# Three element-wise operations of a state-space layer with a quantized MLP, moved from GpSimd to VectorE

## What is computed

```python
xn = layernorm(x)                                    # x: 4 x 2048 x 2048, f32
s  = ((scan(xn) + xn * Dp) * sigmoid(xn @ Wg + bg)) @ Wo
def bit_linear(x, w, b, dim_in):
    x_norm = simple_rms_norm(x, dim_in)              # row / rms(row) / sqrt(dim_in)
    x_q = activation_quant(x_norm)                   # round(x * 127 / max|row|), back to scale
    w_q = sign(w) * mean(abs(w))
    return x_q @ w_q.T + b
h  = gelu(bit_linear(xn, w1, b1, 2048))              # 2048 -> 8192
g  = silu(bit_linear(h,  w2, b2, 8192))              # 8192 -> 2048
out = x + s * g
```

## Time and profile before

| quantity | value |
| --- | --- |
| runs of the kernel before | 3167.06 and 3173.94 us, median 3170.5 us |
| the profiled execution's own time | 3172.91 us |
| span of its slowest core, core 3 | 3171.3 us |
| spans of all cores | 3150.4 to 3171.3 us |
| busy in that span | PE 1671.7, DVE 1452.8, ACT 936.9, POOL 593.2 us |

### The profile page before, as it was taken

How to read it: one execution, slowest core, us unless ns; L and a number is a source line. 1 busy time by engine, 2 the same in 40 slices (tenths; PEclk the granted TensorE clock), 3 DMA queues, 4 the chain that set the end, 5 groups by cost and what they waited for, 6 DMA issues and landing times.

```text
span 3171.3 us, 23059 instructions; the slowest of 8 cores (3150.4 to 3171.3 us)
## 1 busy us (share of the span) xinstructions
PE 1671.7 (53%) x6432; PEld 649.0 (20%) x6432; DVE 1452.8 (46%) x1416; ACT 936.9 (30%) x1045; POOL 593.2 (19%) x264
## 2 busy tenths in 40 slices
PE   2222264555418747777777777600000079999933
PEld 1100021111103313323333222200000024444411
DVE  3655526777713312222222222279999623333354
ACT  2211008777701100012222222211111264645122
POOL 0000004555510000013333333333333100000000
PEclk9999995565559968878888888855555589999955
DMA  4100027777760151122222222133333355555155
GB/s 121 54 27 27 0 31 164 159 173 168 166 111 3 24 96 40 40 94 104 92 90 106 100 106 100 73 113 113 119 113 116 142 186 199 191 174 193 41 159 173
DMA packets 129723, 340.84 MB, mean 107 GB/s; under 512 B 17664, under 2 KB 68992, under 8 KB 114080
## 3 DMA queue, kind: packets, MB, share of 16 engines
q1 hardware_dynamic: 114144, 287.78, 26.5%
q0 software_dynamic: 15456, 51.58, 10.0%
HBM read 290.10 MB, written 100.66 MB: 123 GB/s over the span
## 4 chain that ended last, share of the span: by engine, by line
PE 44%; DVE 18%; DMA 14%; issue 12%; ACT 5%; another core or an unknown queue 3%; SPq 1%; DVEq 1%; POOL 0%; ACTq 0%; POOLq 0%
PE pmA L821 15%; PE pmA L1017 14%; PE pmA L736 4%; DMA p_s<-s1Tsc 4%; PE pmA L700 4%; DMA p_w<-w1T 3%; DMA s1Tsc<-p_w 3%; DVE p_t L950 3%; DVE p_t L957 2%; PE pmC L401 2%; ACT p_w L614 1%; DVE p_v L954 1%; DMA out<-p_og 1%; ACT p_dmp L605 1%
## 5 line engine op out<-in xcount | busy, mean ns | idle before, releaser
L1017 PE MATMUL pmA<-p_k2g,p_s 128*128 128x512 bf16 x2048 | 460.3, 381 | 489.1 <-ACT p_s L1006 489.1
L821 PE MATMUL pmA<-k1T,p_s 128*128 128x512 bf16 x2048 | 483.8, 395 | 169.4 <-DMA p_s<-s1Tsc 169.4
L1017 PEld LDWEIGHTS pmA<-p_k2g,p_s 128*128 128x128 bf16 x2048 | 191.6, 98 | 758.9 <-issue 550.0
L846 POOL TENSOR_TENSOR p_acs<-p_acs,p_h 128x1024 f32<-128x1024 f32 x63 | 213.2, 3384 | 432.3 <-ACT p_h L836 432.3
L821 PEld LDWEIGHTS pmA<-k1T,p_s 128*128 128x128 bf16 x2048 | 199.1, 101 | 455.1 <-issue 259.1
L829 DVE TENSOR_TENSOR p_h<-pmA,p_a1b 128x512 f32<-128x512 f32 x128 | 88.5, 692 | 381.4 <-PE pmA L821 381.4
L1031 DVE TENSOR_TENSOR p_S<-p_S,pmA 128x1024 f32<-128x1024 f32 x112 | 136.8, 1222 | 260.5 <-PE pmA L1017 260.5
L832 ACT ACTIVATE p_hg<-p_h,p_b1c 128x512 f32<-128x512 f32 x128 | 92.4, 722 | 458.6 <-DVE p_h L829 458.5
L961 DVE SCALAR_TENSOR_TENSOR p_k<-p_t,p_int 128x1024 bf16<-128x1024 f32 x64 | 210.2, 3285 | 11.3 <-DVE p_t L957 11.2
L944 POOL TENSOR_TENSOR p_v<-p_hg,p_c2b 128x1024 f32<-128x1024 f32 x64 | 150.6, 2354 | 305.7 <-DVE p_t L957 276.5
L582 PE MATMUL pmA<-ehl,bsel_t 32*128 32x512 bf16 x256 | 110.8, 572 | 175.9 <-DVE p_d L589 165.3
(11 more groups left out here) (161 smaller groups left out, 1818.7 us busy)
## 6 DMA issues: line engine op xcount, KB each, us to landing
p_w<-w2T SPq DMA_DIRECT2D x64, 1024.0 KB, 5.5
p_w<-w1T POOLq DMA_DIRECT2D x64, 512.0 KB, 8.6
s1Tsc<-p_w SPq DMA_DIRECT2D x256, 128.0 KB, 6.5
p_s<-s1Tsc SPq DMA_DIRECT2D x16, 2048.0 KB, 8.8
hgsc<-p_hg SPq DMA_DIRECT2D x64, 512.0 KB, 2.7
p_hg<-hgsc SPq DMA_DIRECT2D x64, 512.0 KB, 3.6
p_xb<-x_sh SPq DMA_DIRECT2D x16, 1024.0 KB, 7.3
k2Tsc<-p_k SPq DMA_DIRECT2D x64, 256.0 KB, 2.1
```

The source lines that it names most:

```text
L821: bld.op(TE, lambda e, k=k, icl=icl, tc=tc, pb=pb, sb_=sb_: e.matmul(pb[:, 0:512], sb_[:, k * 512 + icl * 128:k * 512 + (icl + 1) * 128], ...
L846: bld.op(GP, lambda e, h2b=h2b: e.tensor_add(acs[:], acs[:], h2b[:]), reads=[(h2b, 0), (h2b, 1), (acs, 0)], writes=[(acs, 0)])
L1017: bld.op(TE, lambda e, ic=ic, ds=ds, tc=tc, pb=pb, kg=kg, s2b=s2b: e.matmul(pb[:, tc * 512:(tc + 1) * 512], s2b[:, ic * 2048 + ds * 128:ic ...
```

## The change

The sum over squares (L841 and L846) and the multiplication by `c2b` (L944) go from GpSimd (`GP`) to VectorE (`VE`). Operands, types, shapes and the place of each call in the code stay as they were, and with them the line numbers.

```diff
                     if ic == 0:
-                        bld.op(GP, lambda e, h2b=h2b: e.tensor_copy(acs[:], h2b[:]),
+                        bld.op(VE, lambda e, h2b=h2b: e.tensor_copy(acs[:], h2b[:]),
...
                     else:
-                        bld.op(GP, lambda e, h2b=h2b: e.tensor_add(acs[:], acs[:], h2b[:]),
+                        bld.op(VE, lambda e, h2b=h2b: e.tensor_add(acs[:], acs[:], h2b[:]),
...
-                bld.op(GP, lambda e, hgb=hgb, vb=vb: e.tensor_mul(
+                bld.op(VE, lambda e, hgb=hgb, vb=vb: e.tensor_mul(
                     vb[:], hgb[:], c2b[:]),
```

## The result

| | before | changed |
| --- | --- | --- |
| median | 3169.7 us (19 runs) | 3194.1 us (20 runs) |
| ratio, 95% interval | | 1.0069 (1.0053 to 1.0085) |
| spans of all cores in the profiled execution | 3150.4 to 3171.3 us | 3169.9 to 3187.4 us |
| busy, slowest core: DVE, POOL | 1452.8, 593.2 us | 1467.5, 228.0 us |

The changed kernel is 0.7% slower: the ratio stands for 22 us (17 to 27), the medians lie 24.3 us apart; the forecast was +25.1 us and 3196 us. In five executions of the changed kernel, and in some of other kernels, cores of one die ran at a lower granted clock and took some 1 to 2% longer; the medians in the table hold them, while the ratio and every median from here on leave them out (the changed kernel's is then 3192.8 us).

What follows compares the result with a forecast made beforehand. VectorE's chain was taken to bound the rounding stage, TensorE's work and weight waits the Gelu stage. Rounding stage +27.5, head −1.1 and tail −1.3 gave +25.1 us, forecast 3196 us, range 3180 to 3216.

Steps and rivals of the forecast that it cites:

- VectorE no longer held by GpSimd: Rounding stage: with L944 off GpSimd, L961 stops waiting and the period falls from 6.82 to 4.67 us, 2.15 per chunk.
- What is added: Rounding stage: L944, two hand-overs and ScalarE's L947 join VectorE's chain, 2.56 us per chunk, making the period 7.23 us.
- Head and tail: Shorter first L944 at the rounding stage's head, −1.1 us; earlier release of `acs` at the Gelu stage's end, −1.3 us.
- Rival A: Rounding stage: round trip to ScalarE stays hidden, 5.82 us per chunk, −64 us, 3107 us; chance 0.04.
- Rival B: Rounding stage: L961's 3.39 us is its own cost, period 9.39 us, +164 us, 3335 us; chance 0.03.
- Gelu stage: First-half L829 comes 1.2 us late against 7.1 us of room, second half has 0.8 us to spare: cost nothing.
- Rival C: Gelu stage: the accumulations hold L829 until TensorE lacks a bank, 1.15 us per chunk, +74 us, 3270 us; chance 0.05.

Runs made afterwards that it cites:

- the three doses: Kernel before, GpSimd's c2b multiplication left out (but for two chunks), replaced by a copy, or kept: periods 4.68, 5.50 and 6.79 us; the first two took 3034.0 and 3077.8 us.
- two more: Changed kernel with the running maximum L848 taken three times per chunk: 3270.4 us, some 78 us above the changed kernel's median.
- the middle placement: Changed kernel with the next chunk's multiplication issued between the second and third repair operations: 3094.3 us, ratio 0.9761 to the kernel before; repeated, 3085.8 us, 0.9759.
- the one ahead of all four: Changed kernel with the next chunk's multiplication issued ahead of the first repair operation: 3097.4 us, ratio 0.9767 to the kernel before.

## Why the prediction was right, point by point

- **VectorE no longer held by GpSimd.** Predicted 2.15 us a chunk from the last chunk of the earlier trace rows; measured with GpSimd silent 6.79 − 4.68 = 2.11. L961 is at 1.23 us in all 64.
- **What is added.** L944 1.23 us, first hand-over 0.13, L947 1.06, second 0.14, together 2.56. Measured: 2.53 (2099.69 to 2102.22). Period 7.20 for 7.23, wait ahead of L950 85.1 us for "some 85 us", first L950 to the last L961's end 458.6 us (2073.25 to 2531.83, core 5) for 460.2. The stage's +27.5 us came out as +25.9, because each of the 63 periods was reckoned some 0.03 us too long.
- **Head and tail.** −1.1 and −1.3, measured −1.1 and −1.3.
- **Rival A** (the round trip stays hidden, 5.82 us a chunk) was refused because of the order in VectorE's queue. With another order it is what happens: 5.79 us. The page of the Trainium skill that would send one that way (GPSIMD Engine Reference, "Engine selection") is not wrong on durations, and GpSimd's work did belong on VectorE here, but only together with a place in the queue.
- **Rival B** (the 3.39 us are L961's own) falls with the three doses.
- **Gelu stage.** The verdict "cost nothing" holds, but not by the step that was given for it, which fails: "An L829 that is 1.2 us late does not stop it", with 7.1 us of room. The room left is 1.1 us, the spare time of the ring through ScalarE; the 0.8 us that the same paragraph reckoned for ScalarE's second half was the limit that mattered, and what goes beyond it is paid for each chunk behind the first of a load, not once a load. The sum came out right because one operation more still fitted; by 7.1 us of room two more would have fitted as well, and they cost 74 us. Rival C's price, 1.15 us for each of the 64 chunks "once L829 is held over 7.1 us", had the wrong threshold and, with 64 chunks instead of three for each of 16 loads, the wrong count.

## What to carry to other kernels

When an operation moves to another engine, its own duration is only half of the question (here 1.14 us a chunk); where it stands in that engine's queue is the other half (here 1.4 us a chunk, from 7.20 to 5.79). A producer moved onto its consumer's engine, with another engine's step between the two, exposes that step's whole round trip, as here, unless the producer is issued ahead by more of the engine's own work than the round trip takes (here 2.5 us from start to start). And before taking "this engine has 60% idle time" as room, walk the ring of waits between its operations and add it up: the room is the difference between the ring and the bound of the stage.

## What the runs showed of the hardware that was not expected

- GpSimd copying one 128x1024 f32 tile from SBUF to SBUF (one input) held VectorE's two-input operation as the multiplication did, for its 1.04 us less 0.2. The Trainium skill states it as a rule of the kinds of access (SBUF — State Buffer, "Who interferes with whom": a VectorE operation with two SBUF inputs contends with a GpSimd operation that reads SBUF), and the trace agrees. The busy time of an engine in such a pair is not its work: 132 of L961's 210 us were waiting.
- A VectorE operation that needs the result of the one just before it starts later than one that doesn't: behind a 0.69 us operation after 0.80 against 0.61 us, behind a 1.23 us operation after 1.40 or 1.33 against 1.14 us. An independent operation set between them filled such a pause, which is why the middle placement gives 5.60 us a chunk and the one ahead of all four 5.79 us.
